# Early tile 0 in its own buffer, run lists by ScalarE's queue, table and indices sooner, in a routed expert kernel on one core

## The reference, cut to what matters

```python
# x: (64, 64, 1024) float32, itok: (64,) condition numbers below 16
W = cond_weights[itok]                                  # (64, 64, 64)
y = einsum('bct,bcd->bdt', x, W)                        # the condition stage
logits = y @ W_gate + b_gate                            # 8 experts
_, top_idx = top_k(logits, 2)
y_all = relu(einsum('bsd,edh->bseh', y, W_e) + b_e)     # W_e: (8, 1024, 1024)
out = x + take_along_axis(y_all, top_idx[..., None], axis=2).mean(axis=2)
```

## Time and profile before

| | |
|---|---|
| runs of the kernel before | 882.76, 883.34, 885.81 us (median 883.34) |
| the profiled execution's own time | 886.63 us |
| its span, first to last instruction | 884.9 us |
| TensorE's mean granted clock | 0.985 |
| DMA traffic | 162.47 MB, mean 184 GB/s |

### The profile page before, as it was taken

One profiled execution on the slowest core, in us unless ns is written; L12 is line 12 of the kernel. 1 busy time (PEld: TensorE's weight loads), 2 busy tenths in 40 slices (PEclk: granted clock), 3 DMA queues, 4 the chain that ended last, 5 costly groups with the idle time before them and its releaser, 6 DMA issues.

```text
span 884.9 us, 16708 instructions
## 1 busy us (share of the span) xinstructions
PE 852.1 (96%) x4154; PEld 675.0 (76%) x4155; DVE 422.4 (48%) x595; ACT 256.5 (29%) x310; POOL 450.0 (51%) x500
## 2 busy tenths in 40 slices
PE   7798799999999999999999999999999999999993
PEld 4354378887888888888888888888888888888882
DVE  6688866836643273335533363336333733333320
ACT  5565412124421251114211331115111511112220
POOL 3002325366467667654665556555655565555311
PEclk9999989999999999999999999999999999999997
DMA  9999698998954695447754495547654665444433
GB/s 336 418 417 378 257 340 253 324 329 255 296 125 107 126 294 120 100 95 203 197 106 90 111 289 98 114 96 225 159 114 96 188 121 104 92 100 99 78 48 47
DMA packets 51034, 162.47 MB, mean 184 GB/s; under 512 B 11594, under 2 KB 11658, under 8 KB 50986
## 3 DMA queue, kind: packets, MB, share of 16 engines
q0 software_dynamic: 24544, 76.74, 40.3%
q1 hardware_dynamic: 20618, 67.79, 20.9%
q10 hardware_dynamic: 5840, 17.57, 5.0%
HBM read 106.74 MB, written 70.52 MB: 200 GB/s over the span
## 4 chain that ended last, share of the span: by engine, by line
PE 88%; DVE 3%; DMA 3%; ACT 2%; issue 1%; another core or an unknown queue 1%; ACTq 0%; POOL 0%; DVEq 0%; POOLq 0%
PE psO L607 85%; DMA y_rows<-ys 3%; PE psO L548 1%; ACT ys L700 1%; DVE turned L855 1%; DMA raw<-in_L_cond_weights 1%; PE psG L560 0%; ACT raw L691 0%; ACTq L703 0%; PE psL L572 0%; DVE run_hot L918 0%; DVE place_hot L910 0%; ACT w_hi L713 0%; POOL out L494 0%
## 5 line engine op out<-in xcount | busy, mean ns | idle before, releaser
L607 PE MATMUL psO<-w_hi,a_hi 128*128 (+1 forms) x1104 | 342.1, 391 | 0.5 <-issue 0.5
L607 PE MATMUL psO<-w_hi,a_lo 128*128 (+1 forms) x1104 | 340.9, 390 | 0.0
L607 PE MATMUL psO<-w_lo,a_hi 128*128 (+1 forms) x1104 | 340.8, 390 | 0.0
L465 POOL DMA_INDIRECT rows<-y_rows,idx_g x248 | 259.9, 1048 | 106.8 <-issue 54.4
L607 PEld LDWEIGHTS psO<-w_hi,a_hi 128*128 128x128 f32 x1104 | 207.2, 188 | 44.5 <-issue 1.7
L607 PEld LDWEIGHTS psO<-w_hi,a_lo 128*128 128x128 f32 x1104 | 207.8, 188 | 43.4
L607 PEld LDWEIGHTS psO<-w_lo,a_hi 128*128 128x128 f32 x1104 | 207.8, 188 | 43.3
L1031 DVE TENSOR_TENSOR a_lo<-ys,a_hi 128x1024 fp32r<-128x1024 f32 x62 | 75.9, 1224 | 115.2 <-ACT a_hi L736 74.9
L724 ACT ACTIVATE ys<-ys 128x1024 f32<-128x1024 f32 x33 | 35.0, 1061 | 259.0 <-DVE ys L993 213.5
L724 ACT ACTIVATE rows<-rows 128x1024 f32<-128x1024 f32 x33 | 35.0, 1060 | 253.0 <-DVE rows L993 205.9
L993 DVE TENSOR_TENSOR ys<-psO,bias 128x1024 f32<-128x1024 f32 x33 | 40.3, 1222 | 124.6 <-PE psO L607 82.3
(11 more groups left out here) (141 smaller groups left out, 331.7 us busy)
## 6 DMA issues: line engine op xcount, KB each, us to landing
raw<-in_L_ffn_W_e SPq DMA_DIRECT2D x56, 512.0 KB
y_rows<-ys ACTq DMA_DIRECT2D x32, 512.0 KB, 7.6
out<-in_x SPq DMA_DIRECT2D x14, 1024.0 KB
rows<-in_x SPq DMA_DIRECT2D x16, 512.0 KB, 11.1
more_x<-in_x SPq DMA_DIRECT2D x16, 512.0 KB, 9.6
bias<-in_L_ffn_b_e SPq DMA_DIRECT2D x8, 512.0 KB
rows<-y_rows,idx_g POOLq DMA_INDIRECT x248
raw<-in_L_ffn_W_e POOLq DMA_DIRECT2D x4, 512.0 KB, 8.8
```

Of the source, the lines that this page charges most:

```text
L465: pool.indirect_dma_start(out=rows[:, slot, a * DQ:(a + 1) * DQ], out_offset=None, in_=y_parts[0:(1 + TOK) * Q, :], in_offset=bass.Indirec ...
L607: last = nc.tensor.matmul(ps[:, h * BANK:(h + 1) * BANK], a[:, p, k * P:(k + 1) * P], w[:, bass.ds(slot + (k * H + h * BANK), BANK)], star ...
```

## The change

- Early tile 0 gets a buffer of its own, `early_f`, and need not wait for expert 0's last split. Its transposition stands behind token tile 24 (before: 28), its rounding behind tile 26 on ScalarE (28), its subtraction behind tile 27 on VectorE (ahead of tile 29).
- Group 5's `fill` is no longer behind token tile 31; it is a hook at step 2 of early product 0, and the other hooks stand up to two steps sooner.
- `logits_out` stands ahead of the next diagonal and split on ScalarE.
- `turn_early(1)` stands ahead of `list_out(5)`, and `early_lo(1)` ahead of `slots(6)`.
- `schedule` stands behind `list_out(7)`, ahead of `finish_early(1)`; the index block stands ahead of `finish_early(3)`; on ScalarE the table read stands ahead of `early_hi(4)`.
- The last group's run lists are written by ScalarE (`last_runs`) instead of SyncE.
- SyncE stores the last eight token tiles from their buffers instead of four, each once its product is done, and makes 12 copies instead of 14. The semaphores of the stores are eight, and later users of those buffers wait for them.
- Tile 8's steps stand between the two pairs of chunks of expert 1's first half, whose split is now unconditional.

The diff, cut to its core:

```diff
@@ -106,6 +106,7 @@
             reach_at = lend("reach_at", [P, KR + 1])
+            early_f = lend("early_f", [P, D])
             o_first = more_x[:, 1:1 + FIRST, :]
@@ -216,7 +217,7 @@
         s_xin = [sem(f"s_xin{i}") for i in range(2 * G)]
-        s_xout = [sem(f"s_xout{i}") for i in range(G)]
+        s_xout = [sem(f"s_xout{i}") for i in range(2 * G)]
         s_yout = [sem(f"s_yout{i}") for i in range(G)]
@@ -240,8 +241,9 @@
-        STORES = range(NTILE - G, NTILE)
-        left = range(0, NTILE - G, 2)
+        X = 2 * G
+        STORES = range(NTILE - X, NTILE)
+        left = range(0, NTILE - X, 2)
@@ -250,7 +252,7 @@
         RANKS = {G * g + 9: g for g in range(NG - 2)}
-        FILL = {G * g + 11: g for g in range(NG - 2)}
+        FILL = {G * g + 11: g for g in range(NG - 3)}
         LIST = {G * g + 12: g for g in range(NG - 3)}
@@ -302,7 +302,8 @@
                     sp.wait_ge(s_xin[n % X], n // X * 16 + 16)
-                    sp.dma_start(out[n * P:(n + 1) * P, :], x_at(n % X)).then_inc(s_xout[n % G], 16)
+                    sp.wait_ge(s_y, n + 1)
+                    sp.dma_start(out[n * P:(n + 1) * P, :], x_at(n % X)).then_inc(s_xout[n % X], 16)
@@ -370,7 +371,6 @@
                 copy(5)
-                table_out(NG - 1)
                 read_first(6)
@@ -457,6 +457,8 @@
                     slot = m % 2
+                    if isinstance(n, int) and n < EARLY + 2:
+                        pool.wait_ge(s_xout[slot], 16)
                     c = pool.value_load(tile_c[0:1, bass.ds(n, 1)], min_val=0, max_val=COLS - 1)
@@ -473,8 +475,12 @@
-                    for j in range(2):
-                        pool.wait_ge(s_copy[j], (t + 1) * 16)
+                    if t < len(left) // 2:
+                        for j in range(2):
+                            pool.wait_ge(s_copy[j], (t + 1) * 16)
+                    else:
+                        for s in range(G):
+                            pool.wait_ge(s_xout[s], 16)
                     if t:
@@ -655,9 +661,9 @@
                         fill(FILL[n])
-                early_products(0, hooks={3: lambda: ranks(NG - 2), 4: lambda: gate(NG - 1, 1, 0),
-                                         5: lambda: gate(NG - 1, 1, 1), 7: lambda: unstack(NG - 1)})
-                early_products(1, hooks={0: lambda: fill(NG - 2), 2: lambda: ranks(NG - 1), 7: lambda: fill(NG - 1)})
+                early_products(0, hooks={2: lambda: fill(NG - 3), 3: lambda: (ranks(NG - 2), gate(NG - 1, 1, 0)),
+                                         4: lambda: gate(NG - 1, 1, 1), 6: lambda: unstack(NG - 1)})
+                early_products(1, hooks={0: lambda: fill(NG - 2), 1: lambda: ranks(NG - 1), 5: lambda: fill(NG - 1)})
                 early_products(2)
@@ -712,8 +718,8 @@
-                def split_hi(h):
-                    for k in range(RAW):
+                def split_hi(h, ks=range(RAW)):
+                    for k in ks:
                         at = ((h + 2) % 4) * HALF + k * H
@@ -727,13 +733,26 @@
                         act.wait_ge(s_mm, t - 1)
-                    nc.scalar.copy(a_hi[:, t % 2, :], early_t).then_inc(s_ahi, 1)
+                    nc.scalar.copy(a_hi[:, t % 2, :], early_t if t else early_f[:, :]).then_inc(s_ahi, 1)
...
                     nc.scalar.copy(a_hi[:, m % 2, :], ys[:, m % 2, :]).then_inc(s_ahi, 1)
+                start_of = [act.alloc_register(f"last{e}") for e in range(E)]
+                def last_runs():
+                    g = NG - 1
+                    act.wait_ge(s_list, g + 1)
+                    act.wait_ge(s_sc[g - 1], LAND)
+                    act.load(start_of, starts[0:1, g, :])
+                    for e in range(E):
+                        to = act.snap(start_of[e], min_val=0, max_val=E * TOK - RUN)
+                        act.dma_start(table[bass.ds(to, RUN), :].rearrange("(k w) o -> k (w o)", k=KR),
+                                      lists[e * KR:(e + 1) * KR, g % 2, :]).then_inc(s_sc[g], 16)
@@ -746,22 +765,21 @@
                     y_out(n)
+                    if n in GATE2:
+                        logits_out(GATE2[n])
                     if n < NTILE - G:
...
                         split_first(SPLITS[n])
-                    if n in GATE2:
-                        logits_out(GATE2[n])
-                    if n == NTILE - 4:
+                    if n == NTILE - 6:
                         early_hi(0)
...
                 early_hi(2)
+                last_runs()
+                early_hi(3)
                 relu(tile(0, 1))
-                early_hi(3)
-                early_hi(4)
-                relu(tile(0, 2))
                 for g in range(NG):
@@ -769,6 +787,8 @@
                                   slots_all).then_inc(s_tab, 16)
+                early_hi(4)
+                relu(tile(0, 2))
                 relu(tile(0, 3))
@@ -801,9 +821,14 @@
                 parts(tile(0, EARLY))
-                ahead(EARLY)
+                split_hi(0, range(2))
+                parts(tile(0, EARLY + 1))
+                split_hi(0, range(2, RAW))
+                act.reg_add(reg, reg, 1)
                 relu(tile(0, EARLY - 1))
-                step(2, 0, always)
+                needed(EARLY)
+                relu(tile(0, EARLY))
+                ahead(EARLY + 1)
                 with act.Fori(2, SURE // 4 - 1, 1) as i:
@@ -868,8 +893,8 @@
-                def split_lo(h):
-                    for k in range(RAW):
+                def split_lo(h, ks=range(RAW)):
+                    for k in ks:
                         at = ((h + 2) % 4) * HALF + k * H
@@ -995,23 +1020,25 @@
                     if t < FIRST:
-                        dve.wait_ge(s_xout[t + 1], 16)
+                        dve.wait_ge(s_xout[G + t + 1], 16)
                     elif t % OS >= 2:
                         dve.wait_ge(s_yout[t % OS], 16 * NG)
+                    else:
+                        dve.wait_ge(s_xout[t % OS + 2], 16)
                     finish(tile(0, t), 0)
...
                     dve.wait_ge(s_yx[t % 2], (t // 2 + 1) * (Q * 16))
-                    if t:
+                    if t == 1:
+                        dve.wait_ge(s_split, KD)
+                    if t > 1:
                         dve.wait_ge(s_alo, t)
-                    else:
-                        dve.wait_ge(s_split, KD)
-                    V.transpose(early_t.rearrange("p (k a i) -> p k a i", k=KD, a=Q),
+                    V.transpose((early_t if t else early_f[:, :]).rearrange("p (k a i) -> p k a i", k=KD, a=Q),
                                 fetched[t % 2].rearrange("p (a k j) -> p k a j", k=KD, a=Q)).then_inc(s_zt, 1)
...
                     dve.wait_ge(s_ahi, t + 1)
-                    V.tensor_tensor(a_lo[:, t % 2, :], early_t, a_hi[:, t % 2, :], ALU.subtract).then_inc(s_alo, 1)
+                    V.tensor_tensor(a_lo[:, t % 2, :], early_t if t else early_f[:, :], a_hi[:, t % 2, :], ALU.subtract).then_inc(s_alo, 1)
@@ -1033,25 +1060,25 @@
                         gate_blocks()
-                    if n == NTILE - 3:
-                        early_lo(0)
                     if n in UNSTACK:
...
                         read_from(FROM[n])
+                    if n == NTILE - 5:
+                        early_lo(0)
                     if n in RANKS:
...
                         split_first(SPLITS[n])
-                    if n == NTILE - 4:
+                    if n == NTILE - 8:
                         turn_early(0)
+                turn_early(1)
                 list_out(NG - 3)
+                early_lo(1)
                 slots(NG - 2)
-                turn_early(1)
-                early_lo(1)
                 choose(NG - 1)
@@ -1060,6 +1087,7 @@
                 list_out(NG - 1)
+                schedule()
                 finish_early(1)
@@ -1069,11 +1097,6 @@
                 read_from(6)
-                schedule()
-                early_out(4, EARLY)
-                finish_early(3)
-                turn_early(5)
-                early_lo(5)
@@ -1092,6 +1115,10 @@
                 dve.sem_inc(s_idx, 1)
+                finish_early(3)
+                turn_early(5)
+                early_lo(5)
+                early_out(4, EARLY)
                 finish_early(4)
@@ -1131,12 +1158,14 @@
-                dve.wait_ge(s_xout[0], 16)
+                turn_rows(tile(0, EARLY + 1))
+                dve.wait_ge(s_xout[G], 16)
                 dve.wait_ge(s_add, FIRST * 16)
-                ahead(EARLY)
-                turn_rows(tile(0, EARLY + 1))
+                split_lo(0, range(2))
                 finish_early(EARLY - 1)
                 parts(tile(0, EARLY + 1))
+                split_lo(0, range(2, RAW))
+                dve.reg_add(reg, reg, 1)
                 returned(tile(0, EARLY + 2))
```

1 line of the change is left out of this document (removed).

## The result

The changed kernel takes 888.43 us (median of 6 runs, 887.92 to 889.31); the kernel before, run beside it, took 885.47 us (882.76 to 885.91). The ratio is 1.0039, with a 95% interval from 1.0026 to 1.0052: slower by 3.0 us, where 2.8 us less was forecast, and outside the range of 877.0 to 885.0. Of the 7.9 us between the forecast of 880.5 and the measured time 2.1 are the base: the forecast started from 883.34, the median of three runs, and all six runs of the kernel before give 885.47. The other 5.8 are the change. The profiled execution has a span of 887.6 us against 884.9. From here on product n is the expert product of tile n, and a stop at tile n is a stretch in which TensorE stands idle ahead of that product.

The account below looks back on a forecast made before the run. TensorE's 664.31 us of expert products bound the kernel, so only the start, early tiles and the 0.51 us stop could gain. 2.7 - 0.4 + 0.5 = 2.8 us off 883.34 gave 880.5 us, range 877.0 to 885.0.

Parts of the forecast that it names:

- The start: First expert product near 107.7 instead of 111.20, product 0 ending at 123.2: TensorE alone 5.2 us ahead.
- bound of 107.2: Earliest forecast start of the first expert product, if ScalarE's earlier logits count fully.
- step 3: In product 0, TensorE waits 1.6 us for group 6's mask and all transposed tiles (112.2 against 113.8).
- The bias: Last of SyncE's backlog; lands at 127 (bounds 124.5 and 129.5), holding finish 0, so the gain falls from 5.2 to 3.7.
- group 7's runs: Ready at 131.9 after the bias, finish 0 and slots 7, against 135.6 before: 3.7 us sooner.
- The clock: Rival, 20%: TensorE's new waits bring a half-rate stretch costing 1.5 to 3 us; total 883 (882.0 to 883.5).
- the one before fill 7: TensorE reaches fill 7, at step 5 of product 1, at 130.6 and waits 1.3 us for group 7's runs.
- schedule() without its cover: The 6.04 us schedule now precedes early tile 3 on VectorE; TensorE waits 1.6, product 3 starts 2.7 sooner.
- The table: Read lands after 11.2 us, index block takes 6.4 ahead of finish 3 and tile 5; TensorE waits 0.4 at tile 5.
- the table block stops the early tiles: Rival, 12%: a late table landing holds VectorE's finish 3 and early tile 5, idling TensorE; 886.5 us, slower.
- Tile 8: Its a_lo follows finish 6 directly, near 194, so TensorE's 0.51 us stop goes: 0.5 gained.
- -2.7 + 0.4: Forecast terms: product 3 starts 2.7 us sooner, then TensorE waits 0.4 us for tile 5 before product 5.

Follow-up runs that it names:

- c_stores: The changed kernel with the four added stores taken back (14 copies, as before) and the later waits for them removed; 1.0027 times the kernel before.
- a_after: The changed kernel run again with no edit; 1.0032 times the kernel before.
- b_bias: The changed kernel with the first bias load issued ahead of SyncE's copies instead of behind two copies and the pad; 1.0007 times the kernel before.
- n_sched_tab: The changed kernel with schedule() and the table block in their old places and the bias load still behind the copies; 887.83 us, 1.0032 times the kernel before.
- j2_bias_sched_tab: Repeat of the changed kernel with the bias load first and schedule() and table block in their old places; 881.36 us, 0.9961 times the kernel before.
- d_sched: The changed kernel with schedule() back behind the slots of tile 6, ahead of the wait for the table; 1.0038 times the kernel before.
- e: The changed kernel with the bias load first and schedule() in its old place, the table block in its new one; 1.0008 times the kernel before.
- e2: Repeat of the changed kernel with bias load first, schedule() in its old place and table block in its new one; 885.30 us, 1.0001 times the kernel before.
- j: The changed kernel with the bias load ahead of the copies and schedule() and the table block in their old places; 0.9954 times the kernel before.
- k: The changed kernel with bias load first and schedule(), table block, tile 8's steps and expert 1's splits in the old order; 0.9954 times the kernel before.
- g_tile8: The changed kernel with tile 8 and expert 1's first split half in the old order on ScalarE and VectorE; 1.0026 times the kernel before.
- k2: Repeat of the changed kernel with bias load first and schedule(), table block and tile 8's steps in their old places; 0.9954 times the kernel before.
- h_before_bias: The kernel before the change with only the first bias load moved ahead of SyncE's copies; 0.9996 times the kernel before.

## Why the prediction was wrong

**The start: right, in part by luck.** First expert product 106.66 (107.7 forecast, and sooner than the bound of 107.2), no half clock there, tile 31's transposition ending at 112.7 (113.8), a wait of 0.99 at step 3 (1.6). Product 0 ended at 122.8 (123.2): the start and the wait gave 1.6 us more than forecast, and the small products within it and the gaps around them took 4.3 us and not 3.0.

**The bias: the step that failed.** "After the change SyncE starts 1.8 us later, two y stores and early tile 2's gather are out of the way, and early tile 3's gather comes into it. I take these as cancelling: 127, bounds 124.5 and 129.5." SyncE's timeline after, which answers to the earlier trace rows:

```profile
94.19 3.90 SPq L326 DMA_DIRECT2D slot_table<-lists  x8
98.19 2.17 SPq L306 DMA_DIRECT2D out<-rows  x3
101.35 3.51 SPq L312 DMA_DIRECT2D first<-slot_table  x4
104.96 0.39 SPq L306 DMA_DIRECT2D out<-more_x  x1
107.68 4.42 SPq L326 DMA_DIRECT2D slot_table<-lists  x8
112.19 1.67 SPq L306 DMA_DIRECT2D out<-more_x  x3
113.90 2.52 SPq L341 DMA_DIRECT2D out<-in_x  x2
116.79 0.56 SPq L363 DMA_DIRECT2D out<-in_x  x1
117.41 1.40 SPq L330 DMA_DIRECT2D bias<-in_L_ffn_b_e  x1
```

SyncE is late by 4.4 us at the bias (117.41 against 112.97) and not by 1.8, and nothing cancels it. The run writes of group 3 go at 94.19 (91.33 before), an added store and a later read ahead of them; their landing is what the read at 101.35 waits for (97.25 before), and it takes until 104.9. So SyncE comes to list 4, ready at 103.2, only at 105.46, and is not waiting for VectorE as it was before; reading the places from `starts` into its registers then took it 2.05 us (0.80 before; 0.75 to 2.11 over all traces). The eight run writes begin at 107.68 instead of 103.23, the three stores at 112.19 instead of 106.88. The prediction took SyncE's delay from list 4 alone (which was 1.0 later, not 1.5 to 2) and priced the added stores at up to 0.5 us on a y store, nothing on SyncE's own order, where they stand ahead of the bias. Their share is 0.6 to 2.8 us by c_stores against the traces with eight stores; the rest is open between the later list and the time of SyncE's own steps. The 13.5 us to its landing were near the pad's 14.0. Landed at 130.9, 1.4 behind even the upper bound, it made group 7's runs ready at 135.7 (131.9 forecast, 135.6 before): 5.1 of the 5.6 us won by product 1 went into one wait.

Two pairs, each within a batch, show the term by itself. In a_after and b_bias the bias lands 9.7 us sooner and 1.0032 becomes 1.0007. In n_sched_tab and j2_bias_sched_tab, with the schedule and the table block in their old places, it lands 7.8 us sooner and 1.0032 becomes 0.9961, with intervals far apart.

**The bias alone does not make the forecast right.** b_bias has it landed 5.6 us sooner than forecast and all the rest of the change, and its interval (0.9991 to 1.0024) leaves out the forecast ratio of 0.9968. What is missing came only with the schedule and the table block both back. The ratios, each to the kernel before in its own batch, with the schedule in its old place:

| | table block in its new place | table block back |
|---|---|---|
| bias late | 1.0038 (d) | 1.0032 (n) |
| bias first | 1.0008, 1.0001 (e, e2) | 0.9954, 0.9961 (j, j2) |

With the bias first, the schedule in its new place (b, 1.0007) did no worse than in its old one. The block back and the schedule in its new place never ran, so whether the block's return suffices without the schedule's stays open.

**The clock: a rival that came true, behind a longer wait.** The forecast gave 20% to a half-clock stretch behind one of the new waits, the one before fill 7 among them, at a price of 1.5 to 3 us. Behind 5.11 us of idling in place of 1.3 it came, from 134 to 141, and cost 2.4 (product 1 to product 2 took 19.4 us, 11.95 before, and 5.1 of the difference is the wait). It is what turns "nothing gained" at group 7's runs into 1.9 us lost at product 3.

**schedule() without its cover: right, and hidden.** Forecast 1.6 us of waiting before product 3. With the bias that late TensorE came by itself at 153.5 and did not wait, tile 3 being ready 0.3 us ahead of it; in other traces with the schedule in this place the wait was there (0.44 in a_after, 0.61 in b, 1.78 in c).

**The table: right in the term, wrong in the rival's condition.** The landing took from 151.73 to 163.1, 11.4 us (11.2 forecast), the block 6.5, tile 5 was ready at 174.5 and TensorE took it at 175.26. The forecast's 0.4 was neither borne out nor refuted: the changed kernel had product 3 at 153.5 and not at 148.95, and b_bias, at 150.2, had no stop before product 5. But the working gave 0 as the price if the table landed sooner, and the rival "the table block stops the early tiles" asked for a late table. In e2, with the schedule in its old place, the table was there before the block began and product 5 stopped 3.20 us, with 2.9 of half clock behind: what it needs is VectorE's two long steps in a row and an early start. The rival's own price had a slip as well. From 162.7, where nothing is gained, to 165.5 it is 2.8 us, and the 3.2 put there counts the 0.4 twice. The Trainium skill, "DMA: Bandwidth & Descriptors", section "Issuing engines are not separate DMA queues", has another issuer save the issuing time alone. The 11.4 us with the runs on ScalarE's queue too, beside 11.2 without them, do not speak against it; other traces with both there had 8.0 (k) to 11.1 us (g), and no run here tests it.

**Tile 8: right, tiles 10 and 11 not seen.** The stop of 0.51 us went (0.7 with the change of neighbours). The new stops of 0.40 and 0.84 us, 1.6 by the starts of the tiles, had no term: that GpSimd's scatters would move from behind the weight loads to ahead of them or among them was not followed.

The sum by measured terms (a minus is time gained): +1.9 in place of -2.7 + 0.4 at products 3 and 5, -0.7 in place of -0.5 at tile 8, +1.6 in place of 0 at tiles 10 and 11, together +2.8 in place of -2.8. Of the difference of 5.6 us, 4.2 are the bias with its clock: group 7's runs 3.8 us later than forecast and 2.4 of half clock, less the waits of 1.6 and 0.4 that did not come.

## What to carry over

When work is added to an engine that issues DMAs, follow every later issue of that engine up to the one that something waits for, and take its new start from the sum, not by letting terms cancel. A small load that the early compute needs is worth trying ahead of bulk copies in the same queue's order; here it was worth 6.5 us (n against j2), and nothing in the kernel before. Work moved ahead of a critical tile must be priced at the earliest start that the rest of the change may give, since there its cover is thinnest. The fast versions here kept the sooner start, put the bias ahead of the copies and took two (j) or three (k) of the moves back.

## What the runs showed of the hardware that was not expected

- A wait of TensorE can cost more than its length. 5.11 us of idling were followed by products at half clock until 141 (2.4 us lost), 3.20 us in e2 by 2.9 us lost, 1.78 us before product 3 in c_stores by 1.7 us lost. The length of the wait did not decide it: waits of 2.14 and 2.24 us before fill 7 had such a stretch behind them (n_sched_tab, g_tile8) and one of 2.26 had none (d_sched); 1.20 and 1.75 us before product 2 (j2, k2) had none.
- A bias of half a megabyte took 13.5 us from issue to landing behind two copies and the pad (13.5 to 14.3 in six traces), and 7.3 us when issued just ahead of them (j2; 6.9 to 8.3 in the nine traces with the new start and the bias first, 9.9 in h_before_bias), on the same queue.
- A scatter issued just ahead of four weight loads made the last of them land 8.9 us after its issue (8.4 to 9.5 in five traces with the scatter ahead or among them); with the scatter behind them the slowest took 5.8 (h_before_bias) to 7.0 us (k).
- The start differs from execution to execution by some microseconds, with the stretches of half clock in it. Over the fifteen traces that share the new start product 1 began between 122.7 and 129.2 (128.8 and 127.7 in the two with the old one), and both ends are traces of the kernel of e. One trace with a poor start hid the table block's price altogether.
